# Four layer normalisations of a small vision tower moved from VectorE to ScalarE, with a per-row bias made by GpSimd

## The reference

```python
h = tok(x)                                        # patches to 1024 x 192
h = h + attnA(_layernorm(h))
h = h + ffn_block(_layernorm(h))                  # attention B, then an MLP M
h = h + attn_over_heads(_layernorm(h))            # the last attention, D
h = h + mixture(_layernorm(h))                    # router R and 32 experts

def _layernorm(x, axis=-1, eps=1e-05):
    m = jnp.mean(x, axis=axis, keepdims=True)
    v = jnp.var(x, axis=axis, keepdims=True)
    return (x - m) / jnp.sqrt(v + eps)
```

## Time and profile before

| | us |
|---|---|
| median of 3 runs | 799.89 (797.1 to 800.64) |
| profiled execution | 803.63, of which the profile's span 801.8 |
| normalisations D0, D1 | about 223 and 295 from the span's start |
| normalisations R0, R1 | about 318 and 360 |
| first expert matmul | about 419 |
| busy: PE, DVE, ACT, POOL | 693.9, 421.6, 234.8, 322.3 |

### The profile page before, as it was taken

How to read it: one execution, slowest core, us unless ns; L and a number is a source line. 1 busy time by engine, 2 the same in 40 slices (tenths; PEclk the granted TensorE clock), 3 DMA queues, 4 the chain that set the end, 5 groups by cost and what they waited for, 6 DMA issues and landing times.

```text
span 801.8 us, 19926 instructions
## 1 busy us (share of the span) xinstructions
PE 693.9 (87%) x6364; PEld 587.1 (73%) x6364; DVE 421.6 (53%) x1247; ACT 234.8 (29%) x671; POOL 322.3 (40%) x260
## 2 busy tenths in 40 slices
PE   5938948898989997894539989999999999999995
PEld 5714645655755785783239879999999999899995
DVE  7675573735578229975943343443444434444442
ACT  3102312123146201101414323334333343334332
POOL 6739020011033402421014355655555555465554
PEclk9957968577989899985559999999999999999998
DMA  9900000000000030014103756464545566456432
GB/s 347 242 1 3 1 3 2 2 2 2 1 1 0 2 117 3 0 54 129 43 18 101 232 141 166 108 161 112 157 109 155 121 188 179 117 110 165 108 54 37
DMA packets 35047, 70.00 MB, mean 87 GB/s; under 512 B 6354, under 2 KB 21299, under 8 KB 34995
## 3 DMA queue, kind: packets, MB, share of 16 engines
q0 software_dynamic: 15840, 17.71, 13.2%
q10 hardware_dynamic: 8064, 33.12, 12.1%
q1 hardware_dynamic: 11090, 18.43, 7.0%
HBM read 59.26 MB, written 9.98 MB: 86 GB/s over the span
## 4 chain that ended last, share of the span: by engine, by line
PE 67%; DVE 13%; DMA 8%; issue 7%; ACT 2%; POOL 1%; POOLq 0%; DVEq 0%; ACTq 0%; another core or an unknown queue 0%; SPq 0%
PE bank L1483 14%; PE bank L1475 10%; PE bank L1478 7%; DMA arena<-normed_rows,fetch_u 6%; PE bank L1331 4%; PE bank L1263 4%; PE bank L1367 3%; PE bank L1209 3%; PE bank L1283 3%; PE bank L1460 3%; PE bank L1347 2%; PE bank L1358 2%; DMA out_dram<-arena,number_u 1%; PE bank L1301 1%; PE bank L1274 1%
## 5 line engine op out<-in xcount | busy, mean ns | idle before, releaser
L622 POOL DMA_INDIRECT out_dram<-arena,number_u x80 | 127.1, 1588 | 42.5 <-issue 28.5
L616 POOL DMA_INDIRECT arena<-normed_rows,fetch_u x80 | 78.3, 979 | 127.5 <-DMA out_dram<-arena,number_u 49.5
L787 ACT ACTIVATE arena<-bank,arena 128x128 f32<-128x128 f32 x234 | 64.6, 375 | 115.9 <-PE bank L1478 115.9
L1170 DVE COPY arena<-bank 128x256 f32<-128x256 f32 x81 | 34.4, 424 | 118.3 <-PE bank L1460 80.5
L1483 PE MATMUL bank<-arena 128*128 128x192 f32 x468 | 83.5, 327 | 0.7 <-ACT arena L787 0.4
L1483 PEld LDWEIGHTS bank<-arena 128*128 128x128 f32 x468 | 75.3, 190 | 1.9 <-ACT arena L787 1.9
L530 POOL TENSOR_SCALAR rstd<-mv 128x4 f32<-128x4 f32 x12 | 2.7, 228 | 168.8 <-DVE mv L874 168.8
L1188 DVE TENSOR_SCALAR arena<-bank,arena 128x192 f32 x80 | 33.4, 418 | 52.1 <-PE bank L1483 45.6
L1475 PE MATMUL bank<-arena 128*128 128x128 f32 x468 | 58.8, 276 | 1.3 <-issue 0.7
L558 POOL TENSOR_TENSOR arena<-arena,v_space 128x2304 f32<-128x2304 f32 x8 | 34.5, 4318 | 62.4 <-DVE arena L1103 62.4
L787 ACT ACTIVATE arena<-bank,w_space 128x128 f32<-128x128 f32 x132 | 37.1, 373 | 73.9 <-PE bank L1478 70.7
(11 more groups left out here) (239 smaller groups left out, 1260.9 us busy)
## 6 DMA issues: line engine op xcount, KB each, us to landing
arena<-in_moe_w_dram ACTq DMA_DIRECT2D x14, 579.0 KB
arena<-in_moe_w_dram ACTq DMA_DIRECT2D x14, 576.0 KB
arena<-in_xf_dram SPq DMA_DIRECT2D x8, 512.0 KB, 9.6
w_space<-in_moe_w_dram ACTq DMA_DIRECT2D x7, 579.0 KB
w2small<-in_moe_w_dram ACTq DMA_DIRECT2D x7, 579.0 KB
w_space<-in_moe_w_dram ACTq DMA_DIRECT2D x7, 576.0 KB
wab<-in_moe_w_dram ACTq DMA_DIRECT2D x7, 576.0 KB
arena<-in_w_dram SPq DMA_DIRECT2D x8, 480.0 KB, 8.9
```

What stands on the lines that cost most here:

```text
L616: pool.indirect_dma_start(out=mo_stage[:, s * ROWN:(s + 1) * ROWN], out_offset=None, in_=normed_rows, in_offset=bass.IndirectOffsetOnAxis( ...
L622: pool.indirect_dma_start(out=out, out_offset=bass.IndirectOffsetOnAxis(ap=number_u[:, s:s + 1], axis=0), in_=mo_res[:, s * D:(s + 1) * D] ...
L787: nc.scalar.activation(mo_hT[:, m, :], bank[2 + m][:, 0:P], ACT.Gelu, bias=b1[:, m:m + 1]).then_inc(free[2 + m], 1)
L1170: nc.vector.tensor_copy(mo_xT.rearrange("p k t -> p (k t)"), bank[1][:, 0:2 * P]).then_inc(free[1], 1)
```

## The change

DVE no longer normalises in D and R; for A, z, B and M it does so as before. ACT does it, with `Identity` of `scale * x + bias`, where the scale is `rstd` and the bias is a new tile `shifted`, both one number per row. POOL makes `shifted` as -mean times rstd, with two more small operations behind the two it had, and raises `ln_rstd` only behind them. Each of the four small operations ends before the next starts (`link`). ACT's part stands where the steps `put D n` and `norm R n` stand in the list.

```diff
@@ ln_rstd, on POOL
-                nc.gpsimd.tensor_tensor(out=rstd[:, s], in0=rstd[:, s], in1=minus_half[:, s], op=ALU.pow).then_inc(sem("ln_rstd"), 1)
+                ins = nc.gpsimd.tensor_tensor(out=rstd[:, s], in0=rstd[:, s], in1=minus_half[:, s], op=ALU.pow)
+                if L in "DR":
+                    link(ins)
+                    link(nc.gpsimd.tensor_scalar(out=shifted[:, s], in0=mv[:, s, 0:1].rearrange("p t o -> p (t o)"), scalar1=-1.0, scalar2=None, op0=ALU.mult))
+                    ins = nc.gpsimd.tensor_tensor(out=shifted[:, s], in0=shifted[:, s], in1=rstd[:, s], op=ALU.mult)
+                ins.then_inc(sem("ln_rstd"), 1)
@@ on ACT
+            LN = [(L, n) for step_name, L, n in ORDER if step_name == "ln"]
+
+            def normalized(L, n, dst):
+                act.wait_ge(sem("ln_rstd"), LN.index((L, n)) + 1)
+                for t in range(4 * n, 4 * n + 4):
+                    nc.scalar.activation(dst[:, t, 0:D], h[:, t, :], ACT.Identity, scale=rstd[:, t:t + 1], bias=shifted[:, t:t + 1]).then_inc(sem(f"normed_{L}"), 1)
...
+                elif step_name == "put" and L == "D":
+                    normalized("D", n, xn)
                 elif step_name == "norm":
+                    normalized("R", n, xrow)
                     transposed_rows(*GROUPS[n])
@@ on DVE
-            def normalize_rows(n):
-                dve.wait_ge(sem("ln_rstd"), ln["R", n])
-                for t in range(*GROUPS[n]):
-                    ts(out=xrow[:, t, 0:D], in0=h[:, t, :], scalar1=mv[:, t, 0:1], scalar2=rstd[:, t:t + 1],
-                       op0=ALU.subtract, op1=ALU.mult).then_inc(sem("normed_R"), 1)
...
-                elif step_name == "put":
+                elif step_name == "put" and L != "D":
                     layernorm(L, n)
...
-                elif step_name == "norm":
-                    normalize_rows(n)
```

More of the change, by code:

```diff
@@ L195, in vit_tower @@
         rstd = sb("rstd", [P, T])
+        shifted = sb("shifted", [P, T])
         numbers = sb("numbers", [P, T + 1])
```

## The result

The changed kernel takes 806.88 us (median of 14 runs, 799.9 to 814.61) against 798.85 us of the kernel before (14 runs, 787.34 to 804.48). The ratio is 1.0134, 95% interval 1.009 to 1.0179: slower by 1.3%. That is 8.0 us by the medians, 8.6 us by the means of all runs (±3.2, two standard errors) and 10.7 us by the ratio. The forecast was +3.6 us. The profiled execution took 811.57 us, span 809.7.

What follows compares the result with a forecast made beforehand. PE is busy 87%, but waits among POOL, DVE, ACT and PE at four places decide: 1.22 + 1.01 - 0.35 + 1.76 = +3.64 us, on the median 799.89 giving 803.5 us. The range was 799.5 to 808.0.

Steps and rivals of the forecast that it cites:

- The terms of the queues: Delays and gains at D0, D1, R0 and R1 from moving the normalisation to ACT, summed to +3.64 us.
- POOL's bias: Two more small POOL operations make `ln_rstd` 0.61 us later, with bounds 0.3 and 1.3.
- A tile on ACT: Price of normalising one tile on ACT: 0.54 us, four in 1.86 against DVE's 1.25.
- D0: Later bias and slower tiles delay PE's transposes, ACT's copies and L1358 there: +1.22 us.
- D1: ACT's four tiles hold up the store of the heads, for which DVE's L1085 waits: +1.01 us.
- R0: DVE is freed of 1.25 us but then waits for ACT's copy of the queries: -0.35 us.
- R1: ACT's tiles stand behind the second copy of result rows and delay the transposes' copies: +1.76 us.
- Theory 1: Set up for the experiments: queues cost the forecast 4 us; PE's longer pause at D0 prolongs the low clock, costing the rest.
- The clock was a rival: PE's added idle time drops the clock at D1, and at D0 in more executions: +5 to +7 us total, chance 0.20.
- Cover that I had not seen: Cheap ACT tiles and PE slack behind D0 and D1 leave +0.5 to +1.5; both no-change cases together 0.15.
- Faster: High clock lasts through the first half's result rows and L1386: -1.6 us, 798.3, chance 0.07.
- the full 1.25 us come at R0: DVE is the bound, D0 and D1 hide: -1.25 + 1.76, no change; both no-change cases together 0.15.

Runs made afterwards that it cites:

- R alone: Kernel before with only R's two normalisations on ACT, D's on DVE: 1.0056 against the kernel before.
- R alone moved: Kernel before with only R's normalisations on ACT, R1's tiles ahead of the copies of result rows: 1.0012 against the kernel before.
- the two tries: Kernel before with R's (then only R0's) normalisations on ACT, first-half result rows adding h on DVE instead of PE: 0.9972, then 1.0011 against the kernel before.
- D alone: Kernel before with only D's two normalisations on ACT, POOL's bias for D only, R's on DVE: 1.0082 against the kernel before.
- pause alone: Kernel before with two more small POOL operations on a spare tile at D0, DVE normalising everywhere: 1.0033 against the kernel before.
- moved: Changed kernel with D1's tiles split around the store of the heads and R1's ahead of the result rows' copies: 1.0059 against the kernel before.
- the second try: Kernel before with only R0's normalisation on ACT and first-half result rows copied by DVE with h added: 1.0011 against the kernel before.
- the kernel before with PE kept busy: Kernel before with extra identity products on PE at D0, results never read: 0.9991 against the kernel before.
- the three kernels with extra products: Never-read identity products on PE at D0, added to the changed kernel, kernel before, and changed kernel with moved tiles: 1.0051, 0.9991, 1.0029 against the kernel before.

## Why the prediction was wrong

**The terms of the queues were right**, near enough. POOL's bias: 0.61 forecast, 0.64 measured. A tile on ACT: 0.54 and 0.54; four: 1.86 and 1.86. D0: +1.22, measured +1.50, the transposes running at the low clock for the rest. D1: +1.01, measured +1.07. R0: -0.35, measured -0.31. R1: +1.76, measured +1.70 at an equal clock (R alone). The sum is +3.96 instead of +3.64, so the queues explain about half of the 8 to 9 us. That R0 gives back only a third of DVE's 1.25 us, since ACT's copy of the queries is next, was read rightly.

**The step that failed** is in D0: "PE's transposes, ACT's copies and L1358 follow at the old distances: 0.61 + 0.61 = +1.22 us", with everything behind it merely shifted, as PE's chain to 291. So the sum put the clock behind D0 at nothing, and PE's time there is no constant. In six profiles without a longer pause at D0 and without extra products (the kernel before twice, R alone, R alone moved, the two tries) the stretch from D's first products to the third sum over heads took 64.3, 64.4, 64.4, 64.7, 64.7 and 66.5 us. In five with the pause (changed twice, D alone, moved, pause alone) it took 67.2, 68.5, 68.8, 70.6 and 76.5. The means are 64.8 and 70.3: 5.5 us. Not one of the five is as short as the longest of the six. The clock is what differs: it was low for 11 to 14 us of the stretch in the six and for 17 to 38 us in the five, and each is longer by about half of its extra low time. That the pause brings this about is likely by the profiles; by the timed runs of the pause alone it is not shown.

**The clock was lost in other places too.** Each run has its mean granted clock, and twice the missing share of the time is the time at half speed. For the 14 runs of the changed kernel (0.8846) that is 186 us, for the first 35 runs of the kernel before (0.8901) 176 us. Where PE sets the pace, half of the difference is lost. The queues' terms are taken from the stretches above, with nothing for R1 where its tiles were moved. Both together give the measured loss in every one of these kernels, none of which has extra products; each half is good to 1.5 to 3 us:

| kernel | queues | half the extra low time | sum | measured by the means |
|---|---|---|---|---|
| changed | 4.0 | 5.3 | 9.3 | 8.6 (±3.2) |
| D alone | 2.6 | 3.2 | 5.8 | 6.1 (±1.9) |
| R alone | 1.4 | 3.3 | 4.7 | 3.9 (±1.7) |
| pause alone | 1.7 | 0.8 | 2.5 | 2.4 (±1.8) |
| moved | 1.4 | 2.5 | 3.9 | 4.0 (±2.4) |
| R alone, moved | -0.3 | 1.0 | 0.7 | 0.8 (±2.1) |

So the loss is queues and low clock, and nothing else of a size that these runs could show is left. But R alone lost as much clock as D alone, and its D0 is that of the kernel before. Theory 1, which puts all of the lost clock behind D0, is too narrow.

**The clock was a rival,** with 0.20 and +5 to +7 us. Its size was nearly right; its place and its weight were wrong. I looked for it at D1, where the clock in fact stayed up, and argued for D0 that it had fallen there anyway. In the profiles with the pause it fell there too, but came back later (in four of the five) and then fell a second time in M's first layer (in four of the five; in the fifth it had not risen before). A reading went wrong with it: the 6.72 us of the 16 products were taken as their time at the low clock, but the clock rose to 2.4 GHz during them; the whole 16 at the low clock took 8.02. The page "TensorE: Matmul & The Clock Gate" of the Trainium skill, section on HAM oscillation, warns that gaps in PE's work bring the low clock back. The traces agree at D0 in most kernels, but not in the second try, where the same pause left the clock up. And the fall in the kernel before with PE kept busy came without a gap in PE's busy time (8.00 of 8.00 us), which the busy share of the profile cannot explain.

**The other rivals.** Cover that I had not seen did not exist at D0 and D1. "Faster", by a high clock over the first half's result rows, does occur: 8.87 instead of 13.77 us, but in the kernel before too, so it decides nothing between them. (Its sum is written there as 5.2 - 3.6; the -1.6 us is 3.6 less 5.2.) That the full 1.25 us come at R0 is refuted.

**What stays open.** What makes the clock fall and rise is not known from these runs. Where R alone lost its clock is not known either: its profile has 13.7 us at the low clock in the stretch at R1, against 11.9 and 0 in the two of the kernel before, but one profile does not settle it. In the three kernels with extra products the sums by the table's rule fall short of the measured loss by 1.8, 1.7 and 3.1 us, so these products have a cost that I have not found, within the noise for each. The expert loop varied from 389.6 to 397.4 us over all profiles with no order that follows the change; its two shorter values of the changed kernel (389.6, 391.4) were not tested.

## What to carry to other kernels

A move to an idle engine is paid at its place in that engine's queue: ask what stands behind it there and is ready first, and what stands ahead of it and is ready last. Here the same four tiles cost 1.7 us at one place and nothing a few instructions earlier. And a change that moves PE's waits can move the granted clock over long stretches behind them, so price those stretches at both clocks (here the low clock took about as much as the queues did). One profile does not size that: the stretch behind D0 took 67.2 us in one profile of the changed kernel and 76.5 in the other. The mean granted clock of a dozen runs does it better.

## What the runs showed of the hardware

- TensorE's clock stayed at 1.2 GHz through at least 16 us of gapless work by the profile's busy time (L1339 and L1366, 240 to 256 us in the changed kernel). In the kernel before with PE kept busy it fell from 2.4 GHz in 232 to 240 us, while PE was busy for 8.00 of 8.00 us. In the changed kernel the first sums over heads (L1375), from 260 us on, ran at the full clock again.
- An ACTIVATE of 128 x 192 from on-chip memory with a scale and a bias per row took 0.53 to 0.55 us, four in a row 1.86; DVE's tensor-scalar with the same two operands per row took 1.25 us for four.
- Two executions of the kernel before took 13.77 and 8.87 us for one stretch (result rows and logits), with the clock low for 11.9 us of it in the first and not at all in the second.
- In six changed kernels the mean loss of all runs was that of the queues' terms plus half of the extra time at the low clock, to within 1 us (R alone: 1.4 + 3.3 against 3.9).
